# A routed layer whose second-layer rows are scattered with an adding DMA into the output, in place of a scatter to scratch, a gather back and a weighted sum

## What is computed

```python
logits = flat @ Wr
top_vals, top_idx = jax.lax.top_k(logits, TOP_K)          # TOP_K = 2
top_w = jax.nn.softmax(top_vals, axis=-1)
gates = jnp.zeros((N, E), dtype=flat.dtype).at[jnp.arange(N)[:, None], top_idx].add(top_w)
out = jnp.zeros_like(flat)
for e in range(E):
    hdn = jax.nn.gelu(flat @ W1[e] + b1[e], approximate=False)
    y = hdn @ W2[e] + b2[e]
    out = out + gates[:, e:e + 1] * y
# ... and the caller: x = x + out
```

## Time and profile before

| | us |
|---|---|
| timed runs, median of 3 | 1360.15 (1358.65 to 1361.75) |
| profiled execution, its own time | 1373.4 |
| its span, first to last instruction | 1371.7 |
| PE busy in the span | 1316.7 (96%) |
| DVE busy | 736.0 (54%) |
| ACT busy | 461.9 (34%) |
| POOL busy | 350.6 (26%) |
| mean granted TensorE clock | 0.972 of full |

### The profile page before, as it was taken

How to read it: one execution, slowest core, us unless ns; L and a number is a source line. 1 busy time by engine, 2 the same in 40 slices (tenths; PEclk the granted TensorE clock), 3 DMA queues, 4 the chain that set the end, 5 groups by cost and what they waited for, 6 DMA issues and landing times.

```text
span 1371.7 us, 23245 instructions
## 1 busy us (share of the span) xinstructions
PE 1316.7 (96%) x7745; PEld 881.9 (64%) x7746; DVE 736.0 (54%) x1600; ACT 461.9 (34%) x1152; POOL 350.6 (26%) x491
## 2 busy tenths in 40 slices
PE   9999999999989999999998999999999999899991
PEld 4799954455457777777656777777645555666660
DVE  6799955562158888887575333333352011453334
ACT  2699921011045555555312111111332012521110
POOL 4499920000000000000033555555200000314540
PEclk9999999999999999999999999999999999769996
DMA  6000000040010000000242999999420070312326
GB/s 166 32 2 3 2 1 1 0 188 0 0 42 2 1 2 2 2 1 2 69 139 85 338 329 319 316 322 311 156 115 0 0 245 0 129 53 88 104 85 237
DMA packets 83549, 133.32 MB, mean 97 GB/s; under 512 B 11952, under 2 KB 49222, under 8 KB 82687
## 3 DMA queue, kind: packets, MB, share of 16 engines
q1 hardware_dynamic: 69491, 110.29, 24.6%
q0 software_dynamic: 12176, 18.68, 4.4%
q10 hardware_dynamic: 1788, 3.16, 0.7%
HBM read 117.41 MB, written 29.56 MB: 107 GB/s over the span
## 4 chain that ended last, share of the span: by engine, by line
PE 45%; DVE 3%; DMA 1%; issue 1%; ACT 0%; SPq 0%; POOL 0%; POOLq 0%; DVEq 0%
PE ps L1377 8%; PE ps L1386 8%; PE ps L1469 6%; PE ps L1535 3%; PE ps L1552 3%; PE ps L1519 2%; PE ps L1514 2%; PE ps L123 2%; PE ps L1367 1%; PE ps L1571 1%; PE ps L1486 1%; PE ps L1412 1%; DMA b_r<-y 1%; PE ps L1527 1%; PE ps L1464 1%; PE ps L164 1%
## 5 line engine op out<-in xcount | busy, mean ns | idle before, releaser
L1298 POOL TENSOR_TENSOR b_x<-b_x,b_r 125x512 f32<-125x512 f32 x10 | 12.7, 1271 | 526.5 <-DVE b_r L1769 526.5
L1377 PEld LDWEIGHTS ps<-b_r 128*128 128x128 f32 x1024 | 124.2, 192 | 33.7 <-issue 32.2
L1377 PE MATMUL ps<-b_r 128*128 128x78 f32 x1024 | 122.2, 272 | 1.2 <-DVE b_r L1751 1.2
L1386 PE MATMUL ps<-b_r 128*78 128x512 f32 x256 | 120.3, 592 | 0.0
L659 PE MATMUL ps<-b_r 125*125 125x160 f32 x660 | 117.3, 314 | 0.1
L568 ACT ACTIVATE b_r<-b_r 125x125 f32<-125x125 f32 x330 | 106.8, 390 | 0.4 <-issue 0.2
L1651 ACT ACTIVATE b_r<-ps,b_r 128x78 f32<-128x78 f32 x128 | 34.8, 323 | 203.0 <-PE ps L1377 196.7
L1047 PEld LDWEIGHTS ps<-b_r 125*64 125x64 f32 x1600 | 85.3, 136 | 24.6 <-issue 22.8
L1010 PE MATMUL ps<-b_r 64*125 64x417 f32 (+1 forms) x480 | 95.7, 531 | 1.4 <-DVE ps L1139 1.2
L1047 PE MATMUL ps<-b_r 125*64 125x125 f32 x1600 | 94.7, 272 | 1.3 <-ACT b_r L1075 1.3
L659 PEld LDWEIGHTS ps<-b_r 125*125 125x125 f32 x660 | 92.0, 187 | 5.4 <-ACT b_r L568 0.2
(11 more groups left out here) (286 smaller groups left out, 2305.6 us busy)
## 6 DMA issues: line engine op xcount, KB each, us to landing
b_r<-L_ffn_w SPq DMA_DIRECT2D x128, 512.0 KB
b_r<-y SPq DMA_DIRECT2D x20, 512.0 KB, 7.7
b_r<-L_ffn_W SPq DMA_DIRECT2D x2, 4096.0 KB, 20.0
y<-b_r SPq DMA_DIRECT2D x2, 2500.0 KB
rows<-b_r SPq DMA_DIRECT2D x4, 960.0 KB
b_x<-x SPq DMA_DIRECT2D x5, 480.0 KB
out<-b_x ACTq DMA_DIRECT2D x5, 480.0 KB
b_r<-L_ffn_b SPq DMA_DIRECT2D x1, 2048.0 KB, 8.9
```

Source lines behind the costliest of these rows:

```text
L1377: last = pe.matmul(T.ps[:, 2 + r % 2, f * CAP:(f + 1) * CAP], T.ew1[r % WS][:, k, f * 128:(f + 1) * 128], T.ex_t[:, r % 2, k, :], start=(k ...
L1386: last = pe.matmul(T.ps[:CAP, 4 + r % 2, :], T.eh[:, r % 2, f, :], T.ew2[r % WS][:, f, :], start=(f == 0), stop=(f == FK - 1))
```

## The change

The two result rows of a token are no longer stored apart and summed at the end. Instead:

1. `x` is stored to `out` before the block loop, by six DMAs on SP (2.56 MB), and POOL waits for these (`out_stored`) before its loop.
2. Each slot gets its token's gate. The gate is split into three bfloat16 parts (`split_gates`), multiplied with the one-hot matrix on DVE (`gates_placed`), gathered to slots by 20 matmuls on PE (`make_gates`) and summed on DVE (`slot_gates`). `make_choices` and the DVE instructions that built the old scatter numbers are gone; the scatter number is now the token's number.
3. In the loop DVE multiplies the block's rows by their slots' gates, one more instruction for each block, and POOL scatters them into `out` with a DMA that adds (`compute_op=ALU.add`).
4. Two blocks can hold the same token, so a scatter waits until the scatter just before it has landed.
5. The ten loads, the twenty DVE instructions and the ten stores at the end are gone. SP only waits for the last four scatters.
6. `rows1` is stored in the order of token numbers (2 KB pieces) and not by partition (4 to 8 KB pieces). Two `keep_busy` groups of PE change from 24 matmuls to 10 and 6. Four small stores that filled the spare rows of `y1` in `projections` are gone, and some SBUF tables lie elsewhere.

The diff, cut to its core:

```diff
+def split_gates(dve, link, T):
+    rest = T.gate[:]
+    for i in range(3):
+        link(dve.tensor_copy(T.split[:, i], rest))
+        if i < 2:
+            link(dve.tensor_tensor(T.rest[:], rest, T.split[:, i], ALU.subtract))
+            rest = T.rest[:]
+def gates_placed(dve, T, ready):
+    for i in range(3):
+        last = dve.tensor_tensor(T.gate_parts[:, :, :, i, :], T.place[:],
+                                 T.split[:, i].rearrange("p t j -> p j t").unsqueeze(3).to_broadcast([P, TOP, NT, NB]), ALU.mult)
+    last.then_inc(ready, 1)
+def make_gates(pe, T, bank):
+    for t in range(NT):
+        for j in range(TOP):
+            last = pe.matmul(T.ps[:BR, bank, 0:3 * NB], T.place_rows[:, t * TOP + j, :],
+                             T.gate_parts[:, j, t].rearrange("p i b -> p (i b)"),
+                             start=(t + j == 0), stop=(t == NT - 1 and j == TOP - 1))
+    return last
+def slot_gates(dve, link, T, bank):
+    part = [T.ps[:BR, bank, i * NB:(i + 1) * NB] for i in range(3)]
+    link(dve.tensor_copy(T.slot_gate[:], part[2]))
+    link(dve.tensor_tensor(T.slot_gate[:], part[1], T.slot_gate[:], ALU.add))
+    link(dve.tensor_tensor(T.slot_gate[:], part[0], T.slot_gate[:], ALU.add))
...
             for j in range(TOP):
-                spare = A.y1[j * PLACES + NT * P:(j + 1) * PLACES].rearrange("(p t) d -> p (t d)", t=NT)
-                for c0, c1 in ((0, KD * N), (KD * N, NT * D)):
-                    sp.dma_start(spare[:, c0:c1], feats[0:128 - P, 0:c1 - c0]).then_inc(S.rows_filled, 16)
...
-            sp.wait_ge(S.rows_filled, 128)
+            sp.wait_ge(S.rows_filled, 64)
...
             for t0, n in GROUPS[:2]:
                 sp.wait_ge(S.f_rows, t0 + n)
                 for p0, p1 in ((0, 120), (120, P)):
-                    sp.dma_start(A.rows1.rearrange("(p t) d -> p t d", t=NT)[p0:p1, t0:t0 + n], T.rows_b[p0:p1, t0:t0 + n])\
+                    sp.dma_start(A.rows1.rearrange("(t p) d -> p t d", t=NT)[p0:p1, t0:t0 + n], T.rows_b[p0:p1, t0:t0 + n])\
                       .then_inc(S.rows_stored, 16)
+            sp.wait_ge(S.f_rows, NT)
+            for t0, n in GROUPS:
+                for p0, p1 in ((0, 120), (120, P)):
+                    sp.dma_start(A.out.rearrange("(t p) d -> p t d", t=NT)[p0:p1, t0:t0 + n], T.x[p0:p1, t0:t0 + n])\
+                      .then_inc(S.out_stored, 16)
+            sp.wait_ge(S.out_stored, 96)
             sp.wait_ge(S.ry_last, 64)
-            for i in range(NT // 2):
-                for j, rows in enumerate((T.all_a, T.all_d)):
-                    sp.dma_start(rows[:, 2 * i:2 * i + 2],
-                                 A.y1[j * PLACES:(j + 1) * PLACES].rearrange("(p t) d -> p t d", t=NT)[:, 2 * i:2 * i + 2])\
-                      .then_inc(S.y_gathered[i], 16)
...
             def block_scatter(q, r, stored):
-                if r + 1 < 8:
-                    wait_count(pool, S.ry_stored[(r + 1) % 4], q, 16, 16 * ((r + 1) // 4))
-                pool.wait_ge(S.ry_copied, q * 4 + (r + 1))
+                pool.wait_ge(S.ry_scaled, q * 4 + (r + 1))
+                if r > 4:
+                    pool.wait_ge(S.ry_last, 16 * (r - 4))
+                else:
+                    wait_count(pool, S.ry_stored[(r + 3) % 4], q, 16, 16 if r > 0 else 0)
                 place_column(q, r + 1, (r + 1) % 4 if r + 1 < 8 else 4)
-                pool.indirect_dma_start(A.y1, bass.IndirectOffsetOnAxis(ap=T.ey_ids[:, r % 4:r % 4 + 1], axis=0),
-                                        T.ry[:, r % 4, :], None, bounds_check=TOP * PLACES - 1, oob_is_err=False)\
+                pool.indirect_dma_start(A.out, bass.IndirectOffsetOnAxis(ap=T.ey_ids[:, r % 4:r % 4 + 1], axis=0),
+                                        T.ry[:, r % 4, :], None, bounds_check=N - 1, oob_is_err=False, compute_op=ALU.add)\
                     .then_inc(stored, 16)
...
             token_column(0, 0)
             pool.wait_ge(S.rows_stored, 160)
             pool.wait_ge(S.tail_stored, 16)
             for r in range(4):
                 block_turn(0, r)
             pool.wait_ge(S.blocks_ready, 1)
+            pool.wait_ge(S.out_stored, 96)
             loops = loops_of(pool)
             with pool.Fori(0, loops) as q:
...
-            make_choices(pe, T2, 3, BR, T2.place, NB).then_inc(S.table_made, 1)
-            keep_busy(pe, T, 0, 24)
+            keep_busy(pe, T, 0, 10)
+            pe.wait_ge(S.gates_ready, 2)
+            make_gates(pe, T2, 5).then_inc(S.table_made, 1)
+            keep_busy(pe, T, 0, 6)
...
-            out = A.out.rearrange("(t p) d -> p t d", t=NT)
-            for i in range(NT // 2):
-                act.wait_ge(S.out_ready, 2 * i + 2)
-                for p0, p1 in ((0, 120), (120, P)):
-                    act.dma_start(out[p0:p1, 2 * i:2 * i + 2], T.x[p0:p1, 2 * i:2 * i + 2]).then_inc(S.out_stored, 16)
-            act.wait_ge(S.out_stored, 16 * NT)
...
                 wait_count(dve, S.ry_stored[r % SLOTS1], q, 16, 16 * (r // SLOTS1))
                 dve.tensor_tensor(T.ry[:, r % SLOTS1, :], T.ps[:, 6 + r % 2, :],
                                   T.b2_of[:, bass.ds(e, 1), :].rearrange("p o n -> p (o n)"), ALU.add).then_inc(S.ry_copied, 1)
+                dve.wait_ge(S.ry_copied, q * 4 + (r + 1))
+                dve.tensor_scalar(T.ry[:, r % SLOTS1, :], T.ry[:, r % SLOTS1, :], T2.slot_gate[:, bass.ds(q * 4 + r, 1)], None,
+                                  ALU.mult).then_inc(S.ry_scaled, 1)
...
             gates(dve, link, T)
+            split_gates(dve, link, T2)
             dve.wait_ge(S.table_made, 1 + TOP)
             dve.tensor_scalar(T.ids[:, 0:NB], T.ps[:BR, 7, 0:NB], float(N), None, ALU.add).then_inc(S.ids_ready, 1)
-            low, place = T.ids_low[:, 0:NB], T2.place_ids[:, 0:NB]
-            link(dve.tensor_scalar(low, T.ps[:BR, 7, 0:NB], float(N), None, ALU.add))
-            link(dve.tensor_scalar(place, low, float(N), float(TOP * PLACES), ALU.is_ge, ALU.mult))
-            link(dve.tensor_tensor(place, place, low, ALU.add))
-            dve.wait_ge(S.table_made, 2 * TOP)
-            link(dve.scalar_tensor_tensor(out=T2.sids[:, 0:NB], in0=T.ps[:BR, 3, 0:NB], scalar=float(PLACES), in1=place,
-                                          op0=ALU.mult, op1=ALU.add))
+            link(dve.tensor_scalar(T2.sids[:, 0:NB], T.ps[:BR, 7, 0:NB], float(N), None, ALU.add))
             dve.tensor_copy(T.ey_ids[:, 0:1], T2.sids[:, 0:1])
+            gates_placed(dve, T2, S.gates_ready)
...
             dve.wait_ge(S.b11_loaded, 32)
             block_turned(0, 0)
+            dve.wait_ge(S.table_made, 2 + TOP)
+            slot_gates(dve, link, T2, 5)
             end = blocks(dve, block_step)
             block_output(*end)
-            rows = (T.rows_a, T.rows_d)
-            for t in range(NT):
-                dve.wait_ge(S.y_gathered[t // 2], 64)
-                link(dve.scalar_tensor_tensor(out=T.x[:, t, :], in0=rows[0][:, t, :], scalar=T.gate[:, t, 0:1],
-                                              in1=T.x[:, t, :], op0=ALU.mult, op1=ALU.add))
-                dve.scalar_tensor_tensor(out=T.x[:, t, :], in0=rows[1][:, t, :], scalar=T.gate[:, t, 1:2],
-                                         in1=T.x[:, t, :], op0=ALU.mult, op1=ALU.add).then_inc(S.out_ready, 1)
```

More of the change, by code:

```diff
@@ L880, in _ @@
             for j in range(TOP):
-                spare = A.y1[j * PLACES + NT * P:(j + 1) * PLACES].rearrange("(p t) d -> p (t d)", t=NT)
-                for c0, c1 in ((0, KD * N), (KD * N, NT * D)):
-                    sp.dma_start(spare[:, c0:c1], feats[0:128 - P, 0:c1 - c0]).then_inc(S.rows_filled, 16)
-            for j in range(TOP):
                 filled = A.y0[j * PLACES:(j + 1) * PLACES].rearrange("(p t) d -> p (t d)", t=NT)
@@ L1341, in _ @@
             pool.wait_ge(S.f_rows, NT)
-            pool.dma_start(A.rows1.rearrange("(p t) d -> p t d", t=NT)[:, NT - 2:], T.rows_b[:, NT - 2:]).then_inc(S.tail_stored, 16)
+            pool.dma_start(A.rows1.rearrange("(t p) d -> p t d", t=NT)[:, NT - 2:], T.rows_b[:, NT - 2:]).then_inc(S.tail_stored, 16)
             pool.wait_ge(S.ids_ready, 2)
-            pool.wait_ge(S.table_made, 2 * TOP)
             token_column(0, 0)
@@ L1890, in _ @@
             one, other = T.expert_iota[:, 0:E1].unsqueeze(1), T.expert_iota[:, 0:E1].unsqueeze(2)
-            link(dve.scalar_tensor_tensor(out=T2.place_number, in0=T.part_number[:].to_broadcast([P, NT]), scalar=float(NT),
-                                          in1=T.tile_iota[:], op0=ALU.mult, op1=ALU.add))
-            link(dve.tensor_scalar(T2.place_number, T2.place_number, float(NOWHERE - N), None, ALU.add))
+            link(dve.scalar_tensor_tensor(out=T2.place_number, in0=T.tile_iota[:], scalar=float(P),
+                                          in1=T.part_number[:].to_broadcast([P, NT]), op0=ALU.mult, op1=ALU.add))
+            link(dve.tensor_scalar(T2.place_number, T2.place_number, float(EMPTY - N), None, ALU.add))
```

(13 more changed lines are left out.)

## The result

The changed kernel takes 1374.12 us (median of 4 runs, 1373.03 to 1374.94) against 1360.95 of the kernel before beside it (4 runs, 1358.65 to 1362.24): 13.2 us more, ratio 1.0100 with an interval of 1.0084 to 1.0116. I had forecast 16.6 less than before. What came in is the second rival: the 24 adding scatters take far longer than plain ones.

The account below looks back on a forecast made before the run. PE was taken to bound the loop; afterwards the scatter chain: 1245.97 + 105.3 + 0.3 + 3.6 = 1355.2 against 1371.7, 16.5 us less, so 1360.15 became 1343.5 us. Range for 8 in 10: 1336 to 1366.

Parts of the forecast that it names:

- the second rival: Block loop: adding scatters overlap little and their chain becomes the bound; at a 5.1 us landing 1379.7 us; chance 0.20.
- L = 3.6: Block loop: time from an adding scatter's start to its landing, taken as 3.6 us, the middle of 3.5 and 3.7.
- a second packet time for each of 8 rows: Adding scatter: each of an engine's 8 rows costs another 0.127 us packet, 1.0 us on a plain 2.5, giving 3.5.
- The store of the earlier trace: Estimate of the adding scatter's landing: a plain store of twice the bytes (500 KB) landed after 3.7 us.
- The upper bound of 5.1: Adding scatter's landing: read and write one after the other, 3.64 plus 2.5 less the 1.03 issue, 5.1 us.
- The 0.98 that I assumed between landing and start: POOL in the block loop: 0.98 us from a landing to the next scatter's start, with reaction, copy and gap.
- The span ends with a scatter's landing: End of the kernel, a sign in the changed profile: the last scatter's landing closes the span, forecast at 1355.2 us.
- PE's loop keeps its pace of 4.4 us: Block loop, a sign: PE's pace holds because four row buffers absorb 0.19 us of lag per block, 4.3 in all.
- about three periods of slack: POOL's queue in the block loop: the next gather behind the waiting scatter is needed by PE only three blocks later.
- The edits at nothing: Ahead of and in the loop: `x` stores, `rows1` pieces, `split_gates`, gate table and `slot_gates` costed at nothing.
- The cover of the `x` stores: Ahead of the block loop: stores land near 1214, the first gather starts at 1230.37, so 15 us of cover.
- The fourth rival: Block loop: DVE's new instruction delays POOL's issues 0.55 us each, 12.6 more, 1356; with a later loop start, chance 0.05.

Follow-up runs that it names:

- e3: Changed kernel with the copy of the scatter numbers moved ahead of the waits: 1369.44 us, ratio 1.0049 to the kernel before.
- e4: Changed kernel with adding scatters of only 256 of 512 columns, all 128 rows: 1355.84 us, ratio 0.9953 to the kernel before.
- e5: Changed kernel run again unaltered: 1378.45 us, ratio 1.0119 to the kernel before.
- e7: Changed kernel with adding scatters of only 64 of 128 rows, all columns: 1347.96 us, ratio 0.9900 to the kernel before.
- e8: Changed kernel with plain, overwriting scatters of 256 of 512 columns, still one at a time: 1339.63 us, ratio 0.9839 to the kernel before.
- e1: Changed kernel with plain, overwriting scatters instead of adding ones, still one at a time: 1338.36 us, ratio 0.9805 to the kernel before.
- e0: Kernel before run again unaltered, for a second profile: 1359.7 us.
- e2: Changed kernel with adding scatters going in turn to four tables, not waiting for each other: 1345.57 us, ratio 0.9865 to the kernel before.

## Why the prediction was wrong

**The step that failed: "I take their middle, L = 3.6".** Measured, L is 4.8 in the middle and 4.66 as the mean of the 23 landings that a next scatter waited for (5.64 less 0.98). Here it was a size and not a mechanism: the chain has the structure that the sum gave it. The sum's last term, from the last start to the end, was mistaken in kind as well. Counted from the first transposes, so that the clock ahead of the loop is out of it:

| term | as predicted | measured | difference |
|---|---|---|---|
| transposes to first scatter | 11.36 + 0.60 = 12.0 | 12.0 | 0 |
| 23 distances and the last start's 0.3 | 105.6 | 129.8 | +24.2 |
| last start to the end | 3.6 | 7.0 | +3.4 |
| sum | 121.2 | 148.8 | +27.6 |

The timed runs are 1374.1 - 1343.5 = 30.6 us off. 27.6 of it stands in the table. The 3 that remain lie ahead of the loop and in the difference of the profiled execution from the median (0.8). They are within what executions differ by there: six kernels with the same code ahead of the loop (changed, e3, e4, e5, e7, e8) have their first transposes between 1221.3 and 1225.8, and e1, at the lower clock level from 1190 to 1218 us, at 1232.0.

**Why 3.6 was too low.** The 2.5 for a plain scatter was a misreading: it is the median of four landings, two of them of blocks with few tokens. A full block takes 2.8 (e0 and e1, and the full ones among the four), which is 0.3 more. What I left out is the issue: L begins with POOL's own work, and that grew by 0.57. From the earlier trace rows I charged a second packet time for each of 8 rows, 1.0 us, and the engines paid 1.1 us more. That this fits is partly luck: there are 64 packets more for a scatter, 4 for an engine, and so each cost more than the 0.127 us that I had. These make 2.5 + 0.3 + 0.6 + 1.1 = 4.5; that they add up one after the other is an estimate, and the remaining 0.3 is not split further. The store of the earlier trace rows moves twice the bytes but reads nothing back from DRAM and issues no list of rows, so it was a neighbour in bytes alone. The upper bound of 5.1, a read and a write one after the other, was the nearer one.

The Trainium skill (DMA: Bandwidth & Descriptors, Anatomy of one DMA) fits a DMA of POOL as 2.0 us plus bytes at 436 GB/s. Its estimate of 3.2 us for the doubled bytes is 1.6 under the measured 4.8. For the plain scatters it holds to 0.2 us: 2.6 against 2.8, and its 0.3 us for 128 KB is what e8 against e1 shows. For adding scatters the 128 KB cost 1.0 to 1.1 us.

**The cost of a landing in a chain.** The 0.98 that I assumed between landing and start held: it is 0.92 to 1.01 in 22 of the 23 turns, 0.98 in the mean. e3 shows that I had it for a doubtful reason, since the copy is not what fills it.

**"The span ends with a scatter's landing".** It does not. The last scatter belongs to a block with 18 tokens and lands 3.5 us after its start of 1364.63, at 1368.1, which by luck is near my 3.6. What ends last is a DRAIN of POOL's queue, at the end of the program's block. Here it is in the changed kernel, then in e1, then in the kernel before:

```profile
L1254 POOLq DRAIN  x1: 6930/6930/6930, 1364.4 to 1364.4; - x1
```

```profile
L1254 POOLq DRAIN  x1: 6350/6350/6350, 1339.9 to 1339.9; - x1
```

```profile
L1222 POOLq DRAIN  x1: 6353/6353/6353, 1344.5 to 1344.5; - x1
```

It begins just ahead of the last issue, and is over 5.1 us after that issue ends, whether the scatter adds or not and whether it moves 512 columns or 256 (e8 has 6350 too). In the kernel before it was over at 1350.8, beneath the loads of the end, where I didn't see it. So of the 3.4 us that the end is late, 0.6 are the longer issue; the other 2.8 would have come with a plain scatter as well. What POOL does in the DRAIN isn't known.

**"PE's loop keeps its pace of 4.4 us", since the lag "is taken up by the four buffers".** At 0.19 us of lag for each block it might have been so; at 1.25 it was not. And the buffers of finished rows were the wrong cover: what ran out first were the gathers, which stand on POOL behind the waiting scatter. The prediction named this queue and gave it "about three periods of slack". In e0 the gather that is issued at 1306.2 has its transposes at 1314.0; of these 7.8 us the gather takes 3.5, so the slack was 4.3 us, one period. PE's waits cost nothing by themselves, since each scatter started within 1.01 us of the landing before it, the last one within 1.32.

**The edits at nothing.** The gate table and `split_gates` cost nothing, as predicted: from the last products of the block count (1218.0 before, 1203.3 in e0, 1207.1 changed, 1206.1 in e5) to the first gather it is 12.3 and 12.0 us before, 11.9 in the changed kernel and in e5. DVE's multiplication took 0.49 and not 0.55 us. The cover of the `x` stores was wrongly sized: the last store of `rows1` (POOL's) landed after 3.7 us before and takes 13.7 now (1202.8 to 1216.5), beside the `x` stores. The first gather waits for it, and starts at 1219.02. So 2.5 us of cover were left and not 15. In e2, with twice those stores, the wait was still covered (first gather at 1218.03), but that gather took 8.8 us to land beside them, and PE waited for it.

**The fourth rival** named the right symptom, POOL's issues beyond 1.1 us, for the wrong cause. They grew by 0.57, but e1 has the same DVE instructions and issues in 1.02. The adding lengthens them. That POOL's small copy of token numbers (L1343) takes 0.74 instead of 0.19 goes with it: it starts 1.06 us into an issue that lasts 1.59, and in e1 it has 0.21 again.

## What to carry to other kernels

A wait that puts DMAs in a row turns their latency into a pace: price it as (issue + transfer + the way to the next start, 0.98 us here) times the number, and give the unmeasured latency its upper bound when the break-even (here L = 4.29) lies inside the bounds. Before serializing, ask which transfers can really collide; here 7 of 23 waits were needed, and that turned 13 us lost into 16 us won. Look what else is issued from the queue that waits, since it moves to the same pace. And look in the trace for what ends beneath a tail before you take the tail away, since it can become the end.

## What the runs showed of the hardware

- An indirect DMA that adds (fp32, 128 rows of 2 KB, SBUF to DRAM) lands 4.8 us after its start; without the adding it is 2.8. The issue on POOL is 1.59 against 1.02 us, the same with 256 columns, and 1.46 with 64 rows.
- In full blocks its landing goes by bytes: 3.6 to 3.9 us in the chain with 128 KB, the same for 128 rows of 1 KB and for 64 rows of 2 KB. The blocks with few tokens don't fit in: from a scatter's start to the copy that waited for its landing it is 4.7 us with 43 or 52 tokens (at most 104 KB), but 3.7 with 29 and 3.5 with 3. So bytes alone don't set it, and it isn't a straight line in the rows; how the rows lie on the 16 engines was not looked at.
- Adding scatters to different tables, of which each overlaps the next one's issue by 0.1 to 1.1 us, don't become longer (4.8 us in e2). Gathers beside adding scatters do: 4.1 us in the changed kernel and in e2, 3.4 beside plain ones (e0, e1) and beside adding ones of 64 rows (e7).
- A scatter that adds has 64 more packets than a plain one of 128 rows (4976 and 3440 for 24 scatters and the same gathers).
- The DRAIN of POOL's queue at the end lasts 5.1 us beyond the last issue (6.93 us in all after an adding scatter, 6.35 after a plain one).
- The same kernel's profiled execution had 28 us at half clock ahead of the loop once (0.50 from 1190 to 1218 us) and about 10 us the other time (0.50 from 1200 to 1210), with PE busy for 34.8 of the 40 us before 1190 in both. Its first transposes came 15 us apart.
